# A two-layer transformer on one core: softmax rows of four heads times 32 queries, and the dense part's weights loaded through GpSimd's queue

## What is computed

```
# layer 0: 8 query heads of 64, one shared key/value head, then a dense part of 2048
h   = rmsnorm(x) * (ln1_w * (1 + cond @ ln1_tw.T))
q, k, v = rope(h @ Wq.T), rope(h @ Wk.T), h @ Wv.T
x   = x + softmax(q @ k.T / sqrt(64)) @ v @ Wo.T          # per sequence and head
h   = rmsnorm(x) * (ln2_w * (1 + cond @ ln2_tw.T))
x   = x + (silu(h @ Wg.T) * (h @ Wu.T)) @ Wd.T            # the dense part
# layer 1: 16 query heads of 32, 4 key/value heads from a latent of 128
h   = layernorm(x) * (1 + scale) + shift                  # from cond @ W_ada.T
k, v = (h @ Wkd.T) @ Wku.T, (h @ Wkd.T) @ Wvu.T
out = x + softmax(rope(q) @ rope(k).T / sqrt(32)) @ v @ Wo.T
```

## Time and profile before

| | us |
|---|---|
| median of 3 runs | 859.61 (858.96 to 860.92) |
| the profiled execution | 855.91 |
| its span | 854.1 |
| PE busy | 834.2 (98%) |
| PE weight loads busy | 685.0 (80%) |
| DVE busy | 596.8 (70%) |
| ACT busy | 442.7 (52%) |
| POOL busy | 404.5 (47%) |

### The profile page before, as it was taken

One profiled execution on the slowest core, in us unless ns is written; L12 is line 12 of the kernel. 1 busy time (PEld: TensorE's weight loads), 2 busy tenths in 40 slices (PEclk: granted clock), 3 DMA queues, 4 the chain that ended last, 5 costly groups with the idle time before them and its releaser, 6 DMA issues.

```text
span 854.1 us, 15629 instructions
## 1 busy us (share of the span) xinstructions
PE 834.2 (98%) x5940; PEld 685.0 (80%) x5940; DVE 596.8 (70%) x877; ACT 442.7 (52%) x819; POOL 404.5 (47%) x318
## 2 busy tenths in 40 slices
PE   9899999999999999999999999999999999999997
PEld 6687788788788788787787888887878878887885
DVE  6787466666665765766556787876867857668886
ACT  4666455455345455444447556465364454544662
POOL 2566545545544445446455646354444443531431
DMA  9902533533533533523623546446255254240001
GB/s 347 365 25 75 167 115 102 179 121 108 179 102 102 179 103 114 164 82 126 211 103 118 164 143 187 142 150 189 91 164 159 96 167 163 79 130 14 26 27 38
DMA packets 114298, 113.54 MB, mean 133 GB/s; under 512 B 57520, under 2 KB 80048, under 8 KB 114224
## 3 DMA queue, kind: packets, MB, share of 16 engines
q1 hardware_dynamic: 113504, 112.45, 41.1%
q10 hardware_dynamic: 720, 0.09, 0.1%
HBM read 88.15 MB, written 24.38 MB: 132 GB/s over the span
## 4 chain that ended last, share of the span: by engine, by line
PE 75%; issue 6%; DVE 5%; DMA 5%; POOL 4%; ACT 3%; SPq 1%; POOLq 0%; ACTq 0%; DVEq 0%
PE ps L703 24%; PE ps L705 22%; PE ps L704 22%; DMA turned_q<-tq 1%; DVE ex L1441 1%; DMA wost<-WoT 1%; PE ps L972 1%; PE ps L794 1%; PE ps L740 1%; DMA turned_y<-txy 1%; PE ps L822 1%; ACT yf L1871 1%; DMA qkT<-turned_q 1%; POOL wol L629 1%; DVE u L1405 1%
## 5 line engine op out<-in xcount | busy, mean ns | idle before, releaser
L703 PE MATMUL ps<-h2h,guh 128*128 128x512 f32 x512 | 203.5, 397 | 2.2 <-issue 1.2
L705 PE MATMUL ps<-h2l,guh 128*128 128x512 f32 x512 | 199.7, 390 | 0.0
L704 PE MATMUL ps<-h2h,gul 128*128 128x512 f32 x512 | 199.6, 390 | 0.0
L568 POOL TENSOR_TENSOR gul<-rgu,guh 128x1024 fp32r<-128x1024 f32 x64 | 161.2, 2518 | 69.8 <-ACT guh L1779 69.7
L573 POOL TENSOR_TENSOR wdl<-rwd,wdh 128x512 fp32r<-128x512 f32 x64 | 83.0, 1296 | 139.6 <-ACT wdh L1787 139.6
L1340 DVE TENSOR_TENSOR xres<-ps,xres 128x512 f32<-128x512 f32 x128 | 87.6, 685 | 59.2 <-PE ps L705 58.6
L703 PEld LDWEIGHTS ps<-h2h,guh 128*128 128x128 f32 x512 | 96.0, 188 | 28.6 <-issue 9.0
L705 PEld LDWEIGHTS ps<-h2l,guh 128*128 128x128 f32 x512 | 96.1, 188 | 21.0
L704 PEld LDWEIGHTS ps<-h2h,gul 128*128 128x128 f32 x512 | 96.2, 188 | 19.0
L703 PE MATMUL ps<-wdh,ah 128*128 128x512 f32 x256 | 100.3, 392 | 2.6 <-DVE al L1335 1.4
L704 PE MATMUL ps<-wdh,al 128*128 128x512 f32 x256 | 99.7, 389 | 0.0
(11 more groups left out here) (179 smaller groups left out, 1639.5 us busy)
## 6 DMA issues: line engine op xcount, KB each, us to landing
rgu<-gu SPq DMA_DIRECT2D x64, 512.0 KB, 4.7
rwd<-WdT SPq DMA_DIRECT2D x64, 256.0 KB, 4.1
turned_q<-tq SPq DMA_DIRECT2D x20, 320.0 KB, 2.4
qkT<-turned_q SPq DMA_DIRECT2D x20, 320.0 KB, 3.7
turned_p<-tp SPq DMA_DIRECT2D x9, 512.0 KB, 2.6
pT<-turned_p SPq DMA_DIRECT2D x9, 512.0 KB, 3.9
xt<-xT SPq DMA_DIRECT2D x16, 256.0 KB, 3.5
out<-xres SPq DMA_DIRECT2D x15, 256.0 KB, 3.6
```

What stands on the lines that cost most here:

```text
L568: pool.tensor_tensor(gul[i][:, :], rgu[i][:, :], guh[i][:, :], ALU.subtract).then_inc(m_gul, 1)
L703: pe.matmul(dst, lh, rh, start=start, stop=False)
L704: pe.matmul(dst, ll, rh, start=False, stop=False)
L705: return pe.matmul(dst, lh, rl, start=False, stop=stop)
```

## The change

Scores: one matmul now takes, as weights, 32 queries of four heads of one sequence (128 columns, `qkT[r, 2 * b + h, 0:KT, :]`) on 64 rows (layer 0) or 32 rows (layer 1), and streams that sequence's 64 keys. Before it took 64 queries of one head (64 columns). There are half as many matmuls: 8 in place of 16 for a tile in layer 0, 16 in place of 32 in layer 1. The partitions of the scores are four heads times 32 queries. `qkT` and `qkT1` are held by words of 32 queries, with keys beside the queries, so that they come back from DRAM by `back` in runs of 5 times 32 floats (640 bytes).

Context: values are held once, `v0` and `v1` with the two sequences on 64 partitions each, and each takes one ACT instruction in place of four. In layer 0's head `context` goes from two matmuls on the full array with `bdv` to four on quarters of it with `v0`, into two banks. In layer 1 it is 8 matmuls of 256 columns in place of 16 of 128. The waits of `context` and `x2_T` are changed to suit the banks.

Weights of the dense part: SP's `mlp` is gone. POOL issues the load for step n + 2 right behind its own low part of step n. The first four loads are issued by POOL behind `low_wo`.

Order: in `FILL1` stages -1 and 0 are dealt out anew (as many pieces in sum). ACT's `norm1(0)` goes behind the first pieces of stage s = 15, DVE's `turn_y(0)` behind the second. In stage u = 9 DVE adds two pieces before `rope_mul1(10)` in place of after it. The first zeroed tile is `zeros`, for `keep_warm` alone.

The diff, cut to its core:

```diff
-FILL1 = {-1: (4, 4, 0, 4, 0), **{u: (4, 2, 2, 2, 2) for u in range(0, 9)}, 9: (0, 0, 0, 0, 0)}
+FILL1 = {-1: (4, 2, 2, 2, 2), 0: (4, 2, 4, 2, 0), **{u: (4, 2, 2, 2, 2) for u in range(1, 9)}}
...
-            qkT = sb("qkT", [P, KT + 1, P], into=l0)
+            qkT = sb("qkT", [P, W, KT + 1, B32], into=l0)
...
-                back_in_rows(qkT, dq0[t, :, :], ld_q0)
+                back(qkT, dq0[t, :, :], ld_q0)
...
 # POOL, low_gu
                 pool.tensor_tensor(gul[i][:, :], rgu[i][:, :], guh[i][:, :], ALU.subtract).then_inc(m_gul, 1)
+                if n + 2 < NN:
+                    pool.wait_ge(m_gul, n + 1)
+                    pool.dma_start(rgu[i][:, :], gu[(n + 2) % NG, :, :]).then_inc(ld_gu[i], 16)
 # POOL, low_wd
                 pool.tensor_tensor(wdl[r][:, :], rwd[n % 2][:, :], wdh[r][:, :], ALU.subtract).then_inc(m_wdl, 1)
+                if n + 2 < NN:
+                    g = (n + 2) % NG
+                    pool.wait_ge(m_wdl, n + 1)
+                    pool.dma_start(rwd[n % 2][:, :], WdT[g * P:(g + 1) * P, :]).then_inc(ld_wd[n % 2], 16)
...
             low_wo()
+            for n in range(2):
+                pool.dma_start(rgu[n][:, :], gu[n, :, :]).then_inc(ld_gu[n], 16)
+                pool.dma_start(rwd[n][:, :], WdT[n * P:(n + 1) * P, :]).then_inc(ld_wd[n], 16)
...
 # PE, scores
-                for j in range(KT):
+                for h in range(2):
                     for b in range(2):
                         for i in range(2):
-                            r, q = slice(HD0 * i, HD0 * (i + 1)), slice(S * b, S * (b + 1))
-                            mm = pe.matmul(ps[q, XB[2 + rows_of(t, b, i)], S * j:S * (j + 1)], qkT[r, j, q],
-                                           qkT[r, KT, q], start=True, stop=True)
+                            r, n = slice(HD0 * i, HD0 * (i + 1)), 2 * h + b
+                            mm = pe.matmul(ps[:, XB[2 + i], S * n:S * (n + 1)], of_all(qkT[r, 2 * b + h, 0:KT, :]),
+                                           qkT[r, 2 * b:2 * b + 2, KT, :], start=True, stop=True, tile_position=(HD0 * i, 0))
...
 # PE, context, t <= HEAD
-                    mm = pe.matmul(ps[:, BG, 256 * b:256 * (b + 1)], bdv[t % 2][:, b, :],
-                                   pT[:, 2 * b:2 * b + 2, :, :], start=True, stop=True)
+                    for i in range(2):
+                        r = slice(S * b, S * (b + 1))
+                        mm = pe.matmul(ps[HD0 * i:HD0 * (i + 1), ctx_bank(t, b), 0:256], v0[t % 2][r, :],
+                                       pT[r, :, 2 * i:2 * i + 2, :],
+                                       start=True, stop=True, tile_position=(S * b, HD0 * i))
...
 # PE, scores1, t < 15
-                            r, q = slice(HD1 * j, HD1 * (j + 1)), slice(S * b, S * (b + 1))
-                            mm = pe.matmul(ps[q, banks1(t)[j], S * g:S * (g + 1)], qkT1[r, g, q], qkT1[r, KT, q],
-                                           start=True, stop=True, tile_position=(HD1 * j, S * b))
+                            q, k = of_all(qkT1[r, 2 * b + h, 0:KT, :]), qkT1[r, 2 * b:2 * b + 2, KT, :]
+                            mm = pe.matmul(ps[:, banks1(t)[j], S * n:S * (n + 1)], q, k, start=True, stop=True,
+                                           tile_position=(HD1 * j, 0))
...
 # DVE, stage u == TAIL (9)
+                if u == TAIL:
+                    fill(pieces, 2)
                 if in_layer(u + 1):
                     rope_mul1(u + 1)
                 if u == TAIL:
-                    fill(pieces, 2)
                     probs_T1(u)
...
 # ACT, stage s == 15
-                if s == NT - 1:
-                    norm1(0)
                 fill(pieces, f1)
                 if s > HEAD and in_layer(s + 1):
                     values(s + 1)
+                if s == NT - 1:
+                    norm1(0)
```

More of the change, by code:

```diff
@@ L156, in build @@
         qkr1 = sb("qkr1", [P, D + P])
-        v1 = [sb(f"v1_{i}", [P, 2, KT, HD1]) for i in range(2)]
-        sb("pad2", [P, 4 * KT * HD1])
-        qkT1 = sb("qkT1", [P, KT + 1, P])
+        v1 = [sb(f"v1_{i}", [P, KT, HD1]) for i in range(2)]
+        sb("pad2", [P, 6 * KT * HD1])
+        qkT1 = sb("qkT1", [P, W, KT + 1, B32])
         ex1 = sb("ex1", [P, KT, 4, S])
@@ L514, in _ @@
         def _(pool):
-            for i in range(2):
-                pool.memset(bdv[i][:, :, :], 0.0).then_inc(zeroed, 1)
+            pool.memset(zeros[:, :], 0.0).then_inc(zeroed, 1)
             pool.memset(minus_half[:, :], -0.5).then_inc(zeroed, 1)
-            pool.wait_ge(zeroed, 3)
+            pool.wait_ge(zeroed, 2)
             def inv_root(col, signal):
@@ L739, in keep_warm @@
                 for _ in range(n):
[L740 to L741 removed]
+                    pe.matmul(ps[:, BD[1], 0:2 * P], zeros[:, 0:P], zeros[:, :], start=True, stop=True)
             def first_qkv(t):
@@ L815, in context @@
                     wait(pe, a_cl, t)
+                    wait(pe, a_gf, t - 1)
                 else:
@@ L994, in context1 @@
                 for b in range(2):
-                    for r in range(2):
-                        for j in range(KT):
-                            rows, heads = slice(S * r, S * (r + 1)), pT1[S * r:S * (r + 1), :, 2 * j:2 * j + 2, :]
-                            to = ctx_view1(banks1(t)[2 + r])[HD1 * j:HD1 * (j + 1), :, 2 * b:2 * b + 2, :]
-                            mm = pe.matmul(to, v1[t % 2][rows, b, j, :],
-                                           heads[:, 2 * b:2 * b + 2].rearrange("p w i f -> p i w f"),
-                                           start=True, stop=True, tile_position=(S * r, HD1 * j))
+                    for j in range(KT):
+                        r = slice(S * b, S * (b + 1))
+                        mm = pe.matmul(ps[HD1 * j:HD1 * (j + 1), banks1(t)[2 + b], 0:256], v1[t % 2][r, j, :],
+                                       pT1[r, :, 2 * j:2 * j + 2, :],
+                                       start=True, stop=True, tile_position=(S * b, HD1 * j))
                 mm.then_inc(b_ctx, 1)
@@ L1033, in context_last @@
                 for b in range(2):
-                    for r in range(2):
-                        for j in range(KT):
-                            rows = slice(S * r, S * (r + 1))
-                            mm = pe.matmul(ps[HD1 * j:HD1 * (j + 1), last_ctx(h) + r, S * b:S * (b + 1)],
-                                           v1[t % 2][rows, b, j, :], pT1[rows, 2 * b:2 * b + 2, 2 * j + h, :],
-                                           start=True, stop=True, tile_position=(S * r, HD1 * j))
+                    for j in range(KT):
+                        r = slice(S * b, S * (b + 1))
+                        mm = pe.matmul(ps[HD1 * j:HD1 * (j + 1), last_ctx(h) + b, 0:P], v1[t % 2][r, j, :],
+                                       pT1[r, :, 2 * j + h, :], start=True, stop=True,
+                                       tile_position=(S * b, HD1 * j))
                 mm.then_inc(b_ctx, 1)
```

167 lines of the change are left out of this document (57 added, 110 removed).

## The result

The changed kernel takes 869.51 us (median of 4 runs, 867.1 to 873.44), the one before 859.29 in the same comparison. The ratio is 1.0128, 95% interval 1.0099 to 1.0157: 1.3% slower, where 862.3 was forecast with a range up to 868. The profiled execution is 871.26 us with a span of 869.4, 15.3 more than the 854.1 of before. A part of this is the granted clock of single executions: it was 0.996 in two of the four runs (867.77 and 867.10 us) and 0.990 and 0.988 in the others (871.26 and 873.44). The kernel before, run again 89 times beside the later experiments, took 859.5 us in the mean of its 30 executions at 0.996; at that clock the change is some 8 us slower.

A forecast was written before the change was run, and what follows sets the result against it. PE's own instruction stream was taken to bound the kernel. Scores +9.1, context -1.4 and stalls -5.0 gave +2.7 us on the median of 859.61, so 862.3 us, range 847.5 to 868.

The forecast's parts named there:

- Scores: Score matmuls on PE: rounds paced by 128-column weight loads, +6.7 us in layer 0, +2.4 in layer 1, together +9.1.
- the lower end: Lower bound for the scores: a round set by the stream alone, 64 columns in about 0.053 us, giving -3.4 us.
- Rival 1: Scores on PE: the stream sets the pace, a round is 0.053 us, total 849.8 us; chance 0.34.
- Context of the head: Layer 0's head: context on quarters, 0.59 us in place of 1.13, less array-split changes; -1.4 us over tiles 1 to 4.
- Stalls: Four PE waits, (a) to (d), behind things the change moves: together -5.0 us, range -5.0 to 0.
- (a): PE's 1.0 us wait at 411.87 for ACT's silu, with ACT stood in `norm1(0)`; to go.
- (c): PE's 1.4 us wait at 701.67 for DVE's `al`, traced to a late down weight; to go with POOL's issuing.
- (d): PE's 1.1 us wait at 775.87 for DVE's add, which stood behind `rope_mul1(10)`; to go.
- (b): Layer 1's scores waiting twice for queries from DRAM, 1.5 us in sum, first at u = 0; to go.
- Loads from POOL: POOL issuing the dense part's weights, 0.43 us each: hidden in head and middle, 0 us, range 0 to +6.
- Rival 4: POOL comes late: issues of 1.74 us or more, +4.0 in the head plus middle waits, 868.3 us or more; chance 0.05.

The follow-up runs named there:

- a_keys_twice: The changed kernel with each matmul of layer 0's scores streaming its keys twice (128 columns in place of 64): 870.89 us, ratio 1.0129.
- b_order: The kernel before with only the three changes of order (`norm1(0)`, `turn_y(0)`, two pieces ahead of `rope_mul1(10)`): 856.25 us, ratio 0.9955.
- experiment 1: Also written `a_fill_back`: the changed kernel with the kernel before's deal of the pieces (`FILL1`): 870.83 us, ratio 1.0142.
- a_sp_loads: Also experiment 4: the changed kernel with SP issuing the dense part's loads as before, POOL's issues taken out: 860.96 us, ratio 1.0036.
- experiment 5: The changed kernel with SP issuing only the loads for steps 36 to 44, around the turn of the layers: 861.17 us, ratio 1.0024.
- experiment 2: Also written `a_out_later`: the changed kernel with POOL making the low part of layer 1's output weights behind stage -1's last two pieces: 866.38 us, ratio 1.0097.
- experiment 7: `a_sp_loads` with small POOL instructions at each issue's place: one (861.24 us), one more at every fourth place (864.01), or two (876.39).
- experiment 8: Each POOL load issued behind POOL's next instruction, in three kernels: `a_issue_later` 868.17 us, `b_pool_issue_later` 864.43, `a_issue_out_later` 866.8.
- b_pool_issue_later: The kernel before with POOL issuing the dense part's loads, each behind POOL's next instruction: 864.43 us, ratio 1.0054.
- a_sp_busy: `a_sp_loads` with POOL doing one small unused instruction at each place where it issued a load: 861.24 us, ratio 1.0022.
- a_sp_busy_more: `a_sp_busy` with a second small POOL instruction at every fourth place: 864.01 us, ratio 1.0036.
- a_issue_out_later: The changed kernel with the edits of both `a_issue_later` and experiment 2: 866.8 us, ratio 1.0083.
- a_issue_later: The changed kernel with each load issued by POOL behind the next instruction that POOL has to do anyway: 868.17 us, ratio 1.0089.
- b_pool_loads: The kernel before with POOL issuing the dense part's loads and nothing else of the change: 867.81 us, ratio 1.0088.

## Why the prediction was wrong

By the ratios the change's 1.28%, 11.0 us, divides into 7.3 for the attention (forecast 9.1 - 1.4 = 7.7), -4.2 for order and deal (forecast -5.0 with the stalls) and 7.9 for the loads (forecast 0). The sum is 11.0 by the way it is formed, since each kernel stands between two others; that the loads alone cost 7.6 on the kernel before (0.88%) is an independent check. The direction was right and two of three terms too; one step failed.

- **Scores.** Layer 0: the starts spread over 0.84 (forecast 0.76). A stage of its middle is 32.91 us long, from 108.69 to 141.60, against 32.50: +0.41 for a forecast of 0.42. Layer 1: 0.85 (forecast 0.78). The weight load is 196 ns in layer 0 and 186 in layer 1 in the mean (forecast 188). That a record's length tells the stream's, by which the lower end had 0.053 us for 64 columns, does not hold: the records of layer 0's scores are 272 ns in the change with 64 columns and 272 in `a_keys_twice` with 128. Rival 1, a round paced by the stream, is refuted by the spread, and by `a_keys_twice` by itself.
- **Context of the head.** 0.60 us to the next start, as forecast. But with PE sooner there, three tiles' scores wait 0.34 each for ACT's copy of the queries: 1.0 us (shown above), which takes back most of the 1.4. The step named no such wait.
- **Stalls.** (a), (c) and (d) are gone in the trace of the change. `b_order`, which does (a) and (d) alone, measures -0.45% (-0.24 to -0.65), 2.1 us or more, as much as they were worth, though in its profiled execution PE waits 2.35 us for probabilities and 2.01 for queries. (b) at u = 0 went as argued, with the transposition two pieces sooner: with the old deal it is there (2.18 us in experiment 1), with the new it is not. (c) was credited to the loads from POOL; it is gone in `a_sp_loads` too, so it did not need POOL's queue.
- **Loads from POOL: the failed step.** "In the middle a stage holds six issues, 2.6 us, on an engine that is idle half the time. [...] I take 0". In the head this held: POOL's wait before `rope_sum(2)` fell from 2.95 to 2.51 and PE does not wait there. An issue was mis-sized, 0.56 to 0.59 us and with the wait for POOL's own low part 0.92, not 0.43. The larger error is that the half idle time was a mean over stages, and that the other transfers were left out of the sum. At the turn POOL also makes `low_w1_out`, 5.0 us, and works from about 460 to 480 with hardly a gap; what waits behind it there is the inverse root that DVE needs, and beside it is `al`. Four issues in that stretch took what was left. Experiments 4 and 5 show that the issues at the turn cost it. Experiments 2 and 7 show the wait for the inverse root, the change and 8 the hold on `al`, and `b_pool_issue_later` a transfer that lands late beside POOL's. How the 7.9 us divide among these is not shown.
- **Rival 4** named 868.3 or more for "POOL comes late" and had 0.05. Its time was near, by another path: it wanted issues of 1.74 us and a loss of 4 us in the head.
- **The clock.** No step had it. A wait of 2 to 4 us at the turn is followed by some 5 us at half the clock in the change and in experiment 1, so a small lateness is charged twice. In the change the clock falls again behind the wait at 532.40 (0.83 from 530 to 540). It does not follow each time: `a_out_later` waited 2.8 us for queries with the clock at 1.00. In the head the change's profiled execution was granted 0.75 from 30 to 40 us and lost 1.1 us against that of `a_out_later`, which has the same head and kept 1.00; this too belongs to the execution.

The turn's losses can be laid side by side with what PE waited between the two landmarks, over the kernel before's 2.5 us, and with what the clock took (5 us times the missing share of each window of 5 us):

| kernel | issued by; POOL held a place | `al` | ratio | turn's loss, us | PE's waits | clock |
|---|---|---|---|---|---|---|
| `a_sp_loads` | SP, 0 | 1.37 | 1.0036 | -1.8 | -2.2 | 0 |
| `a_sp_busy` | SP, 0.81 | 1.07 | 1.0022 | 2.0 | 0.2 | 1.7 |
| `a_sp_busy_more` | SP, 0.96 | 1.06 | 1.0036 | 4.8 | 1.2 | 3.4 |
| `a_issue_out_later` | POOL, 0.57 | 0.69 | 1.0083 | 2.2 | 0.1 | 1.7 |
| `a_out_later` | POOL, 0.92 | 1.50 | 1.0097 | 2.7 | 1.8 | 0 |
| `a_issue_later` | POOL, 0.57 | 8.40 | 1.0089 | 5.2 | 3.0 | 1.7 |
| the change | POOL, 0.92 | 8.79 | 1.0128 | 8.4 | 3.4 | 5.1 |
| `a_fill_back` | POOL, 0.92 | 1.34 | 1.0142 | 9.8 | 2.8 | 6.9 |
| `b_pool_loads` | POOL, 0.92 | 1.11 | 1.0088 | 6.6 | 5.1 | 1.7 |
| `b_pool_issue_later` | POOL, 0.57 | 1.12 | 1.0054 | 8.0 | 5.8 | 3.4 |

The last two columns add up to the loss within 1.2 us: PE's waits and the clock behind them are what is lost there. The hold on `al` is not needed for it: three kernels lose 6.6 to 9.8 without one. Beside `a_issue_out_later` the hold goes with 3.0 us more, in one execution each, and the ratios of those two cannot be told apart.

**What stays open** is how the cost divides between POOL's time and the route. With about as much of POOL's time on SP's route the ratios are 1.0022 and 1.0036; `a_issue_out_later` and `a_out_later`, with POOL's route and no hold (1.0083, 1.0097), stand 0.6% above them in the mean, some 5 us. On the kernel before, the route with 0.57 a place and no hold costs 0.54%, 4.6 us. So the route, with what an issue holds beside DVE, may well be the larger part of the 7.9. The queries that landed 2.6 us late in experiment 8 show one way; none of these kernels has the route without POOL's time. In `a_issue_out_later` PE waits three times for probabilities from DRAM, 3.0 us in sum.

## What to carry to other kernels

A step that is moved to an engine "idle half the time" has to be laid into the engine's fullest stretch, not its mean: list that engine's timeline where one-off work (here the next layer's weights) meets the steady work, and ask what small result is queued behind it. Price an issue with the wait for its own data. Ask too which transfers that others wait for will now run beside the moved ones, where they were ahead of them in one queue. Before a loss in one profiled execution is explained, see how much of it is a lower clock. When an edit bundles order and resources, the order alone may be the whole gain: here it gave 0.5%, and the rest cost 1.8%.

## What the runs showed of the hardware

- A DVE instruction with two operands in SBUF can be held beyond one instruction of POOL: 8.79 and 8.78 us over six that follow each other without a gap (in the change and `a_keys_twice`) and 8.40 us over an issue and five (`a_issue_later`), for 0.69 undisturbed. The Trainium skill ("SBUF — State Buffer", section Who interferes with whom) calls the ports that the two share an exclusive lock. That speaks for one instruction's length; the rows with 1.37 us agree, those with 8 go beyond it. Held to the end, `al` had started 0.33 us behind the start of POOL's instruction or during an issue; at 0.36 (`a_out_later`) and at 0.47 to 0.79 behind, it got in behind one instruction, and in `a_issue_out_later`, during an issue too, it was not held. What decides is open.
- A plain transfer issued by POOL takes 0.56 to 0.59 us of it in the mean, against 0.43 on SP, and landed no later: 3.9 and 3.0 us from issue to landing for gate and down weights, where SP's took 4.0 and 4.1 in `a_sp_loads`. The kernel before has 4.7 and 4.1. No run here shows when the first byte came.
- Queries of 320 KB sent back through SP's queue landed after 3.6 us in the kernel before and after 6.2 us at the same place in `b_pool_issue_later`, with two loads issued by POOL within 1.3 us of them.
